# Attention and experts on one core: where q's high parts and the fourth key maximum stand in the order of a block

## The chip, the cores and the metric

The kernel runs on one core of a Trainium2 chip. The metric is the device time of one execution in microseconds (us), taken as the median of several runs. The core has TensorE (PE: matmuls, with its weight loads shown as PEld), VectorE (DVE), ScalarE (ACT), GpSimd (POOL) and SyncE (SP, which issues most DMAs). Each engine works through its own instructions in order, and waits on semaphores for the others.

## What is computed

Two things follow each other, both on x of shape (2, 1024, 256).

```python
# cross attention: 16 heads of 64; queries are the normed x, keys and values the normed context (77) and the normed x
q = lat @ Wq;  k, v = split(concat([x, lat]) @ Wkv)      # per batch: 1024 queries, 1101 keys
attn = softmax(q @ k.T * 64 ** -0.5);  x = x + (attn @ v) @ Wout
# mixture of experts: 32 experts, 4 of them per token through 4 of 8 groups, capacity 320, and one shared expert
x = x + shared(xn) + sum(gate * expert(xn))
```

The change touches only the order of instructions in the attention.

## The kernel before, in words

**Blocks.** The attention is cut into 8 turns T (4 pairs of heads and 2 batches make 16 pairs of heads, two a turn), and each turn into four blocks d = 0 to 3. A block is one pair of heads and 512 queries. I number blocks 4T + d, so 0 to 31. A block walks through two heads (h = 0, 1) and nine key tiles (kt = 0 to 8), which makes 18 slots. In each slot PE makes the scores `st` (a pair of matmuls, lines 939 and 943), ACT takes their exp (L1597, which also frees the PSUM bank for the next scores but one), and POOL adds it to the running sum of the head (`add`, L751).

**Splits.** Projections and scores are made in split float32: a high part and a low part. For q, PE makes the product (`q`, L811, into one of the two banks ps_t), ACT writes four high parts (`hi`, parts 0 to 3, L1574), and then DVE writes two low parts (`lo`, two instructions of L1306), which also frees the bank.

**Maxima.** Softmax needs the row maximum before the exp. For each head and each 128 queries PE multiplies q's high part with all keys (`max`, three matmuls of L916 into the three banks ps_m), and DVE reduces them (L1314) into one column of `neg`. There is only one such set of banks, so each `max` group on PE waits for the reduction of the one before. After four maxima PE turns the columns into a row (`row`, one matmul, L922, into a bank ps_t), and DVE multiplies it in (L1321) where the second score matmul of the head reads it. Right behind the row of head 1 PE makes the sums of the block before (`sum`, L961), whose reciprocal DVE takes (L1325); POOL multiplies it in (`norm`, L756), and PE makes the output (`out`, L974).

**Banks.** The tiles `k`, `q`, `v`, `row`, `sum`, `out` and some routing tiles take the two banks ps_t in turn ("jobs"), and each waits until the job two before it has been read.

**Order.** The order is written out by hand in `turn_slots()`: `after[h, kt]` lists what follows slot (h, kt). `whole_plan()` strings the slots together, and every engine goes through the same plan and picks its own part. Blocks with d odd are *project* blocks: in them the keys, q and values of the next pair of heads are made (`k`, `q`, `v`). Blocks with d even are *light* blocks: only q of the next 512 queries is made. Routing work of the experts is hung on fixed slots of later blocks by `extra_events()`: ("turned", a tile transposed on PE, with its low part on DVE, L1370, in slot (0, 5) of blocks 20 and 24), ("hot_a", a comparison on DVE, L1136, in slot (0, 5) of block 22), ("best_a", a search for the best four, in slot (0, 5) of block 26), and ("scat", an indirect DMA issued by POOL) in slots (0, 2), (0, 7), (1, 2) and (1, 7) of blocks 24 to 31.

**The weights' low part.** In slot (1, 1) of each light block, behind the reciprocal, DVE subtracts the high part of the next Wq and Wk from their raw values (`w`, L1293: both inputs in SBUF, in `arena` and `arena_r`). The next thing that DVE does is the first reduction for the next block.

Of the kernel before, what the change touches and what calls it, by code (L numbers as in the profile page):

```python
# [48 lines left out]
def turn_slots():  # L49


    slots = []
    for d in range(QUADS):
        n, ahead = (d + 1) % QUADS, -int(d == LAST_D)
        prev, behind = (d - 1) % QUADS, int(d == 0)
        pp = n // 2
        project = n % 2 == 0

        def nxt(*ev):
            return ev, ahead  # L60

        def own(*ev):
            return ev, 0

        def old(*ev):
            return ev, behind

        def values(make, block, kts):
            return [make("av", block, kt) for kt in kts]

        def project_q():
            return [nxt("q", pp, n % 2), nxt("hi", "q", pp, n % 2, (0, 1))]

        def project_k(i):
            return [nxt("k", pp, i), nxt("hi", "k", pp, i, (0, 1))]

        q_again, q_low = nxt("hi", "q", pp, n % 2, (2, 3)), nxt("lo", "q", pp, n % 2)
        k_low = [nxt("lo", "k", pp, i) for i in range(3)]
        first_values = values(own, d, (0, 1, 2))
        more_values = values(own, d, (3, 4, 5))  # L80
        last_values = values(old, prev, (6, 7, 8))
        own_max = [own("max", d, 1, i) for i in range(4)]
        next_max = [nxt("max", n, 0, i) for i in range(4)]
        out = [old("out", prev, i) for i in range(2)]
        after = {(0, 8): [own("row", d, 1), old("sum", prev)],
                 (1, 1): [],
                 (1, 2): [old("norm", prev), next_max[0]],
                 (1, 3): first_values + [next_max[1]],
                 (1, 4): [out[0], next_max[2]],
                 (0, 7): last_values[2:]}  # L90
        if project:
            after[0, 0] = [own_max[0]] + project_k(0) + [own_max[1], k_low[0]]
            after[0, 2] = project_k(2) + [own_max[2], k_low[2]]
            after[0, 3] = project_k(1) + [k_low[1]]
            after[0, 5] = project_q() + [q_again] + last_values[:2] + [q_low, own_max[3]]
            after[1, 5] = [nxt("v", pp, 0), next_max[3]]
            after[1, 6] = more_values + [nxt("row", n, 0), out[1]]
            after[1, 7] = [nxt("v", pp, 1)]
            after[1, 8] = [nxt("v", pp, 2)]
        else:  # L100
            after[0, 0] = [own_max[0]] + project_q()
            after[0, 1] = [own_max[1]]
            after[0, 2] = [q_again]
            after[0, 3] = [own_max[2], q_low]
            after[0, 4] = last_values[:2]
            after[0, 5] = [own_max[3]]
            after[1, 6] = [out[1], next_max[3]]
            after[1, 7] = more_values + [nxt("row", n, 0)]
        if d == 0:
            after[1, 1] = [own("w", 1)] + after[1, 1]  # L110
        if d == 2:
            after[1, 1] = [(("w", 0), -1)] + after[1, 1]
        for h in range(2):
            for kt in range(KEY_TILES):
                slots.append([own("st", d, h, kt)] + ([own("add", d, h, kt)] if kt else []) + after.get((h, kt), []))
    return slots
# [98 lines left out]
def whole_plan():  # L215
# [5 lines left out]
              ("max", 0, 0, 1), ("v", 0, 1), ("max", 0, 0, 2), ("v", 0, 2), ("max", 0, 0, 3), ("row", 0, 0)]  # L221
    plan = [(ev, 0) for ev in before]
    slots, extra = turn_slots(), extra_events()
    ahead = [ev for slot in slots for ev, back in slot if back == -1]
    assert set(ahead) <= set(before), set(ahead) - set(before)
# [1476 lines left out]
```

## Time and profile before

| | |
|---|---|
| Time before | 1634.35 us, median of 3 runs (1633.24 to 1637.85) |
| The profiled execution | 1635.06 us, of which 1633.3 us are the span of the records |
| Attention loop | from about 52 us to 1112 us: 32 blocks, a project block about 36.2 us, a light block 28 to 31 us |
| Busy share of the span | PE 93%, weight loads 65%, DVE 64%, POOL 58%, ACT 49% |
| PE clock | granted clock 0.98 of full speed over the span |

The profiled execution is a single one. Busy PE time is made of overlapping matmuls whose ends are modelled, so for PE the distance from start to start says more than the idle times. A start is given in us from the beginning of the span.

### The profile page before, as it was taken

The page shows a single profiled execution, that of the slowest core. Times are in us where ns is not written, and L with a number is a line of the kernel's source. Part 1 is how long each engine was busy: PE and PEld are TensorE (multiplying, and loading weights), DVE is VectorE, ACT ScalarE, POOL GpSimd, SP SyncE. Part 2 cuts the span into 40 slices and gives each one's busy share as a digit, 9 for nine tenths or more (in the row PEclk, how much of TensorE's full clock was granted, in tenths as well). Part 3 has the DMA queues.
Part 4 walks back from the last instruction along what each step waited for, and adds up shares of the span by engine and source line. Part 5 has one row for each costly group of instructions (what it writes and reads, how often), then busy time and mean ns, then how long its engine had stood idle before and what let it go on. Part 6 is the DMA issues. An engine that isn't in the chain of part 4 may idle for free.

```text
span 1633.3 us, 23810 instructions
## 1 busy us (share of the span) xinstructions
PE 1511.4 (93%) x8086; PEld 1060.9 (65%) x8086; DVE 1051.9 (64%) x1574; ACT 798.7 (49%) x1501; POOL 940.4 (58%) x751
## 2 busy tenths in 40 slices
PE   3899999999999999999999999988889999999995
PEld 2565555555655555555555555546779999999995
DVE  6556666576666665767767776556756666666662
ACT  3345444544454445544454444534336666666662
POOL 4457666676566665665668768784433433344333
PEclk8899999999999999999999999999999999999998
DMA  3033440000000000000011000111246666667664
GB/s 95 22 81 72 101 91 11 24 15 10 24 15 10 15 10 24 15 11 15 10 28 32 27 28 27 36 39 59 85 159 175 188 185 169 174 186 188 169 174 89
DMA packets 99282, 117.93 MB, mean 72 GB/s; under 512 B 10595, under 2 KB 78181, under 8 KB 99173
## 3 DMA queue, kind: packets, MB, share of 16 engines
q1 hardware_dynamic: 82149, 96.97, 20.4%
q0 software_dynamic: 17056, 19.97, 6.3%
q8 instruction: 44, 0.72, 0.2%
q14 instruction: 33, 0.27, 0.1%
HBM read 74.93 MB, written 35.06 MB: 67 GB/s over the span
## 4 chain that ended last, share of the span: by engine, by line
PE 66%; DVE 19%; ACT 8%; POOL 3%; issue 3%; DMA 1%; SPq 0%; DVEq 0%; ACTq 0%; POOLq 0%
PE ps_o L954 11%; PE ps_t L811 8%; PE ps_m L811 8%; PE ps_st L811 7%; DVE arena_r L1314 7%; PE ps_m L916 7%; PE ps_st L939 5%; PE ps_st L943 4%; ACT arena_r L1574 3%; PE ps_m L848 3%; PE ps_o L848 3%; DVE arena L1325 2%; PE ps_t L974 2%; PE ps_t L1021 2%; PE ps_t L961 2%
## 5 line engine op out<-in xcount | busy, mean ns | idle before, releaser
L751 POOL TENSOR_TENSOR arena<-arena 128x512 f32<-128x512 f32 (+1 forms) x512 | 660.2, 1291 | 337.7 <-ACT arena L1597 300.2
L1597 ACT ACTIVATE arena<-ps_st 128x512 f32<-128x512 f32 (+1 forms) x576 | 329.9, 596 | 460.8 <-PE ps_st L943 426.4
L1314 DVE TENSOR_REDUCE arena_r<-ps_m 128x1 fp32r<-128x1107 f32 x256 | 334.2, 1306 | 182.8 <-PE ps_m L916 180.7
L786 POOL DMA_INDIRECT acc_rows<-arena,ids x96 | 150.8, 1571 | 268.1 <-ACT arena L1660 240.4
L954 PE MATMUL ps_o<-arena 128*64 128x512 f32 (+1 forms) x1152 | 276.5, 606 | 0.0
L939 PE MATMUL ps_st<-arena_r 128*128 128x512 f32 (+1 forms) x576 | 247.2, 429 | 13.9 <-ACT arena L1597 13.9
L943 PE MATMUL ps_st<-arena_r 68*128 68x512 f32 (+2 forms) x576 | 231.1, 401 | 2.5 <-DVE arena_r L1321 1.4
L916 PE MATMUL ps_m<-arena_r 128*128 128x370 f32 x768 | 192.6, 359 | 34.6 <-DVE arena_r L1314 27.1
L916 PEld LDWEIGHTS ps_m<-arena_r 128*128 128x128 f32 x768 | 130.9, 192 | 109.5 <-DVE arena_r L1314 68.5
L939 PEld LDWEIGHTS ps_st<-arena_r 128*128 128x128 f32 (+1 forms) x576 | 106.8, 185 | 108.1 <-ACT arena L1597 83.5
L811 PE MATMUL ps_m<-arena_r 128*128 128x320 f32 (+1 forms) x864 | 164.7, 326 | 2.1 <-DVE arena_r L1404 1.2
L954 PEld LDWEIGHTS ps_o<-arena 128*64 128x64 f32 (+1 forms) x1152 | 71.6, 136 | 139.3 <-issue 131.6
L811 PE MATMUL ps_st<-arena_r 128*128 128x320 f32 (+1 forms) x864 | 159.6, 320 | 0.0
L811 PEld LDWEIGHTS ps_m<-arena_r 128*128 128x128 f32 x864 | 136.1, 190 | 13.5 <-issue 9.8
L1448 DVE TENSOR_TENSOR arena<-arena,ps_st 128x320 f32<-128x320 f32 x128 | 62.1, 485 | 125.1 <-ACT arena L1635 125.1
L811 PEld LDWEIGHTS ps_st<-arena_r 128*128 128x128 f32 x864 | 137.3, 189 | 4.2
L1434 DVE TENSOR_TENSOR arena_r<-arena,arena_r 128x1024 fp32r<-128x1024 f32 x93 | 113.7, 1222 | 15.7 <-ACT arena_r L1622 12.5
L943 PEld LDWEIGHTS ps_st<-arena_r 68*128 68x128 f32 (+2 forms) x576 | 107.0, 186 | 18.1 <-DVE arena_r L1321 10.4
L1325 DVE RECIPROCAL arena<-ps_t 128x512 f32<-128x512 f32 x32 | 107.4, 3357 | 11.7 <-PE ps_t L961 11.7
L811 PE MATMUL ps_t<-arena_r 128*128 128x512 f32 x384 | 105.0, 411 | 4.5 <-DVE arena_r L1303 2.6
L1635 ACT ACTIVATE arena<-ps_m 128x320 f32<-128x320 f32 x128 | 56.3, 440 | 102.7 <-PE ps_st L811 100.4
L1321 DVE TENSOR_TENSOR arena_r<-ps_t,mask 4x512 fp32r<-4x512 f32 x64 | 43.8, 684 | 86.3 <-PE ps_t L922 86.2
(211 smaller groups left out, 1922.7 us busy)
## 6 DMA issues: line engine op xcount, KB each, us to landing
arena<-in_L_ffn_wg_dram SPq DMA_DIRECT2D x32, 512.0 KB, 4.6
arena<-in_L_ffn_wu_dram SPq DMA_DIRECT2D x32, 512.0 KB, 6.3
arena<-in_L_ffn_wd_dram SPq DMA_DIRECT2D x32, 512.0 KB, 3.8
x_slots<-route SPq DMA_DIRECT2D x5, 2176.0 KB, 12.9
arena<-x_slots SPq DMA_DIRECT2D x32, 272.0 KB, 2.7
arena_r<-arena_r SPq DMA_DIRECT2D x30, 275.2 KB, 3.8
arena<-in_L_xattn_Wkv_dram SPq DMA_DIRECT2D x32, 128.0 KB, 2.4
arena<-x_slots SPq DMA_DIRECT2D x32, 68.0 KB, 2.4
```

The source lines that it names most:

```text
L751: pool.tensor_tensor(total, probsT[0:rows, h, 0, :] if kt == 1 else total, probsT[0:rows, h, kt, :], ALU.add).then_inc(added, 1)
L786: pool.indirect_dma_start(out=dst[:, :], in_=y_sb[par][:, c, 0:w], in_offset=None, compute_op=ALU.add, out_offset=bass.IndirectOffsetOnAxi ...
L811: mm = pe.matmul(ps, a, m, start=(n == 0), stop=(n == len(pairs) - 1))
L848: mm = pe.matmul(banks[c], a, m, start=(k == 0 and n == 0), stop=(k == HT - 1 and n == 2))
L916: mm = pe.matmul(ps_m[:, piece, 0:PIECE_W + 1], q1[h][:, c:c + P], k1[pp][h][:, lo:lo + PIECE_W + 1], start=True, stop=True)
L939: pe.matmul(ps_st[0:rows, n % 2, :], k1[pp][h][:, r], q1[h][:, c:c + 512], start=True, stop=False)
L943: pe.matmul(ps_st[0:rows, n % 2, :], k2[pp][h][kr, r], q2[h][kr, c:c + 512], start=False, stop=True).then_inc(st_ready, 1)
L954: mm = pe.matmul(ps_o[ROWK[h], :], vals[0:rows, d // 2, kt, ROWK[h]], probsT[0:rows, h, kt, :], start=(kt == 0), stop=(kt == KT_N - 1), sk ...
L1314: dve.tensor_reduce(neg[h][:, c:c + 1], ps_m[:, :, 0:PIECE_W], AX.XY, ALU.max, negate=True)\
L1325: dve.reciprocal(rinv[:, :], bank[:, :]).then_inc(free, 1)
L1434: dve.tensor_tensor(ws_lo[slot][piece], w_raw[slot][:, piece * W:(piece + 1) * W], ws_hi[slot][piece].bitcast(F32), ALU.subtract).then_inc ...
L1597: act.activation(probsT[0:rows, h, kt, :], ps_st[0:rows, n % 2, :], ACT.Exp).then_inc(exp_done, 1)
```

## The change

The change rewrites two parts of the table `after`, and defines `q_high`, a list of the four high parts of q as four events of one instruction each (before there were two events with two instructions each).

```diff
+        q_high = [nxt("hi", "q", pp, n % 2, (part,)) for part in range(4)]
...
             after[0, 3] = project_k(1) + [k_low[1]]
-            after[0, 5] = project_q() + [q_again] + last_values[:2] + [q_low, own_max[3]]
+            after[0, 4] = [own_max[3]]
+            after[0, 5] = project_q() + [q_again] + last_values[:2] + [q_low]
...
         else:
-            after[0, 0] = [own_max[0]] + project_q()
-            after[0, 1] = [own_max[1]]
-            after[0, 2] = [q_again]
-            after[0, 3] = [own_max[2], q_low]
-            after[0, 4] = last_values[:2]
-            after[0, 5] = [own_max[3]]
+            after[0, 0] = [own_max[0], nxt("q", pp, n % 2)]
+            after[0, 1] = [own_max[1], q_high[0]]
+            after[0, 2] = [q_high[1]]
+            after[0, 3] = [own_max[2]]
+            after[0, 4] = last_values[:2] + q_high[2:]
+            after[0, 5] = [own_max[3], q_low]
```

No instruction is added or removed. Because of two new lines above them, everything stands two lines lower in the changed kernel (L1314 becomes L1316, and so on).

**Project blocks, DVE.** From the third maximum of head 1 to the reciprocal, in block 5. L1303 are low parts of k, L1314 the reductions, L1306 the low parts of q, L1321 the row's multiply. Before:

```order
L1314 TENSOR_REDUCE arena_r<-ps_m 128x1
L1303 TENSOR_TENSOR arena_r<-ps_t,arena_r 64x77 x2
L1303 TENSOR_TENSOR arena_r<-ps_t,arena_r 64x512 x2
L1306 SCALAR_TENSOR_TENSOR arena_r<-ps_t,arena_r 64x512 x2
L1314 TENSOR_REDUCE arena_r<-ps_m 128x1
L1321 TENSOR_TENSOR arena_r<-ps_t,mask 4x512
L1325 RECIPROCAL arena<-ps_t 128x512
```

And in the changed kernel:

```order
L1305 TENSOR_TENSOR arena_r<-ps_t,arena_r 64x512 x2
L1316 TENSOR_REDUCE arena_r<-ps_m 128x1
L1308 SCALAR_TENSOR_TENSOR arena_r<-ps_t,arena_r 64x512 x2
L1323 TENSOR_TENSOR arena_r<-ps_t,mask 4x512
L1327 RECIPROCAL arena<-ps_t 128x512
```

The fourth reduction now stands ahead of q's low parts. On PE its three matmuls stand between the scores (0, 4) and (0, 5); before, they stood behind q and the values (0, 6) and (0, 7).

**Light blocks, ACT.** The exps (L1597) and q's high parts (L1574) from the last exp of the block before, in one light block. Before:

```order
L1597 ACTIVATE arena<-ps_st 128x512
L1574 ACTIVATE arena_r<-ps_t 64x512 x2
L1597 ACTIVATE arena<-ps_st 128x512 x2
L1574 ACTIVATE arena_r<-ps_t 64x512 x2
L1597 ACTIVATE arena<-ps_st 128x512 x5
```

And in the changed kernel:

```order
L1599 ACTIVATE arena<-ps_st 128x512 x2
L1576 ACTIVATE arena_r<-ps_t 64x512
L1599 ACTIVATE arena<-ps_st 128x512
L1576 ACTIVATE arena_r<-ps_t 64x512
L1599 ACTIVATE arena<-ps_st 128x512 x2
L1576 ACTIVATE arena_r<-ps_t 64x512 x2
L1599 ACTIVATE arena<-ps_st 128x512 x3
```

The second exp of the block now stands ahead of all high parts, the third behind one, and the fourth behind two. PE's order in light blocks is the same as before.

**Light blocks, DVE.** The reductions, q's low parts and the row's multiply of one light block. Before:

```order
L1314 TENSOR_REDUCE arena_r<-ps_m 128x1 x3
L1306 SCALAR_TENSOR_TENSOR arena_r<-ps_t,arena_r 64x512 x2
L1314 TENSOR_REDUCE arena_r<-ps_m 128x1
L1321 TENSOR_TENSOR arena_r<-ps_t,mask 4x512
L1325 RECIPROCAL arena<-ps_t 128x512
```

And in the changed kernel:

```order
L1316 TENSOR_REDUCE arena_r<-ps_m 128x1 x4
L1308 SCALAR_TENSOR_TENSOR arena_r<-ps_t,arena_r 64x512 x2
L1323 TENSOR_TENSOR arena_r<-ps_t,mask 4x512
L1327 RECIPROCAL arena<-ps_t 128x512
```

Here q's low parts moved the other way: behind the fourth reduction, right ahead of the row's multiply.

## Rows read from the trace of the kernel before

**Rows 1.** The page, part 1: busy us, share of the span, instructions
```profile
PE 1511.4 (93%) x8086; PEld 1060.9 (65%) x8086; DVE 1051.9 (64%) x1574; ACT 798.7 (49%) x1501; POOL 940.4 (58%) x751
```
**Rows 2.** The waits, attention loop: total us, times, longest us
```profile
PE ps_m L916 <- DVE arena_r L1314: 26.1, 28, 1.9
PE ps_st L939 <- ACT arena L1597: 13.9, 38, 1.3
```
**Rows 3.** The timeline, PE, project block 9: start, us, what, [idle before]
```profile
358.29 0.45 PE L939 MATMUL ps_st<-arena_r 128*77 128x512 f32 x1
...
359.19 0.47 PE L922 MATMUL ps_t<-ident,arena_r 128*128 128x512 f32 x1 [0.21 <-DVE arena_r L1314]
359.59 1.08 PE L961 MATMUL ps_t<-arena,ones 128*64 128x512 f32 x4
```
**Rows 4.** The timeline, DVE, same block
```profile
356.31 1.39 DVE L1306 SCALAR_TENSOR_TENSOR arena_r<-ps_t,arena_r 64x512 fp32r<-64x512 f32 x2 [2.12 <-ACT arena_r L1574]
357.73 1.31 DVE L1314 TENSOR_REDUCE arena_r<-ps_m 128x1 fp32r<-128x1107 f32 x1
```
**Rows 5.** The timeline, PE, light block 10, same place
```profile
391.65 0.45 PE L939 MATMUL ps_st<-arena_r 128*77 128x512 f32 x1
...
392.50 1.08 PE L961 MATMUL ps_t<-arena,ones 128*64 128x512 f32 x4
```
**Rows 6.** Line 1306: what DVE waited for ahead of it, us, times
```profile
  ACT arena_r L1574: 32.2, 15
```
**Rows 7.** The timeline, PE, light block 2, maxima two and three
```profile
120.83 0.40 PE L943 MATMUL ps_st<-arena_r 68*128 68x512 f32 x1
...
122.65 0.50 PE L939 MATMUL ps_st<-arena_r 128*128 128x512 f32 x1 [0.46 <-ACT arena L1597]
...
123.22 0.69 PE L916 MATMUL ps_m<-arena_r 128*128 128x370 f32 x3
```
**Rows 8.** The timeline, DVE and ACT, same stretch
```profile
121.77 1.31 DVE L1314 TENSOR_REDUCE arena_r<-ps_m 128x1 fp32r<-128x1107 f32 x1 [1.05 <-PE ps_m L916]
...
122.00 1.09 ACT L1597 ACTIVATE arena<-ps_st 128x512 f32<-128x512 f32 x2
```
**Rows 9.** The timeline, light block 2, fourth maximum and the sums
```profile
127.46 1.31 DVE L1314 TENSOR_REDUCE arena_r<-ps_m 128x1 fp32r<-128x1107 f32 x1 [0.91 <-PE ps_m L916]
...
130.19 1.08 PE L961 MATMUL ps_t<-arena,ones 128*64 128x512 f32 x4
```
**Rows 10.** The timeline, blocks 20 (two rows) and 22
```profile
721.90 0.69 DVE L1370 TENSOR_TENSOR arena_r<-ps_t,arena_r 128x512 fp32r<-128x512 f32 x1
...
723.29 1.08 PE L961 MATMUL ps_t<-arena,ones 128*64 128x512 f32 x4
...
789.76 1.38 DVE L1136 TENSOR_TENSOR spare<-topf,iota_e 128x512 f32<-128x512 f32 x1
```
**Rows 11.** The timeline, POOL, light block 2, its first adds
```profile
122.68 6.95 POOL L751 TENSOR_TENSOR arena<-arena 128x512 f32<-128x512 f32 x5 [2.66 <-ACT arena L1597]
```
**Rows 12.** The timeline, the weights' low part, blocks 2 and 10
```profile
134.59 1.10 DVE L1293 TENSOR_TENSOR arena_r<-arena,arena_r 128x512 fp32r<-128x512 f32 x1
...
396.90 0.63 DVE L1293 TENSOR_TENSOR arena_r<-arena,arena_r 128x512 fp32r<-128x512 f32 x1
396.93 1.72 POOL L751 TENSOR_TENSOR arena<-arena 128x512 f32<-128x512 f32 x1
```
**Rows 13.** The timeline, blocks 28 (two rows) and 30
```profile
998.16 3.19 DVE L1293 TENSOR_TENSOR arena_r<-arena,arena_r 128x512 fp32r<-128x512 f32 x1
...
1002.63 0.61 PE L916 MATMUL ps_m<-arena_r 128*128 128x370 f32 x2 [1.94 <-DVE arena_r L1314]
...
1069.93 1.10 PE L974 MATMUL ps_t<-wout_sb,arena 128*128 128x256 f32 x4 [1.71 <-POOL arena L756]
```
**Rows 14.** The timeline, PE, third maximum ahead, blocks 6 and 10
```profile
269.87 0.79 PE L916 MATMUL ps_m<-arena_r 128*128 128x370 f32 x3 [1.70 <-DVE arena_r L1314]
...
402.84 0.44 PE L916 MATMUL ps_m<-arena_r 128*128 128x370 f32 x1 [1.38 <-DVE arena_r L1314]
```

## The prediction

> **What bounds the kernel now.** I read the page first: PE is busy 93% of the span, no other engine over 64% [rows 1]. So only PE's own idle time can be won, and an edit that moves no PE work can help only where PE waits. Then the view of waits over the attention loop: PE waits 26.1 us for the reductions of maxima and 13.9 us for exps [rows 2]. Small sums, but the waits are regular, so I went through the timeline of one block of each kind, and looked for the same waits in the others. The reader is to see three chains beside PE: ACT's exps, DVE's reductions, and POOL's adds.
>
> **Project blocks: the fourth maximum.** In block 9 the ninth score pair of head 0 starts at 358.29 and the sums at 359.59: 1.30 us [rows 3]. In light block 10 the same stretch takes 392.50 - 391.65 = 0.85 us [rows 5]. The 0.45 us between them is the row's wait: q's low parts hold DVE from 356.31 for 1.39 us, and only then comes the fourth reduction, 357.73 to 359.04 [rows 4]; the row's matmul starts at 359.19. After the change the reduction stands ahead of q's low parts and ends over 3 us before the row needs it. DVE waits 15 times for q's high parts, 32.2 us together [rows 6]: these are the 15 blocks with d odd that make a next q (block 31 makes none). 15 x 0.45 = **6.7 us less**. Lower bound: the printed idle time, 0.21 x 15 = 3.2 us.
> What is late next? PE's product for q starts one max group later (about 0.6 us), so q's low parts start near 357.0 and end near 358.4. The row's multiply can start near 359.2. The cover is 0.8 us, and it would have to be gone before this costs anything.
>
> **Light blocks, the direct part.** In block 2 PE waits 0.46 us for an exp [rows 7], because two exps stand behind two high parts on ACT and start only at 122.00 [rows 8]. The change removes this wait in 11 blocks (the light ones but 0, 8, 10, 12, 14, where DVE is late instead). But the score pair is followed by the third max group, and that needs the second reduction, which ends at 121.77 + 1.31 = 123.08 [rows 8]. It starts at 123.22 today [rows 7]. So at most 0.14 us can come back, and a max group that had to wait lasts 0.79 [rows 14] where this one lasts 0.69 [rows 7]. Between 0 and 0.14 x 11 = 1.5 us I take **0**.
>
> **Light blocks, q's low parts.** They move behind the fourth reduction. In block 2 this ends at 127.46 + 1.31 = 128.77; 1.39 us more [rows 4], with the usual small overlap, gives about 130.1. The sums use the bank that they free, and start at 130.19 [rows 9]. So they fit by less than 0.1 us: 0 in the plain blocks, and the first thing to check. It doesn't fit where more stands there:
> - Block 20: a turned tile stands between, so the row takes q's bank and the sums the tile's. The tile's low part starts at 721.90 and lasts 0.69; behind q's low parts it ends at 721.90 + 1.38 + 0.69 = 723.97, plus 0.07 until PE sees it, against sums at 723.29 [rows 10]. **0.75 us more.**
> - Block 22: the comparison at 789.76, 1.38 long [rows 10], moves back too. It has two inputs in SBUF and has to get past POOL's adds (below). Between 0.2 and 3.5 us; I take **1.5 us more**.
> - Block 0 is irregular (PE starts cold): between a gain of 0.2 and a loss of 2; **0.7 us more**.
>
> **POOL and the weights' low part.** This part isn't in the diff. The first add of block 2 starts at 122.68, as soon as its second exp is done, and then adds follow each other for 6.95 us [rows 11]: 1.28 each and 0.14 apart. The second exp's scores end at 120.83 + 0.40 [rows 7]; it can start near 121.3 and not at 122.00. So POOL's chain of adds starts 0.7 us earlier. Who waits for it? L1293 has both inputs in SBUF, as the adds have, and the rows show that one waits for the other: 0.63 us in block 10, where it starts 0.03 us before an add, which then takes 1.72 for 1.28; 1.10 in block 2, where it comes into a running add [rows 12]; 3.19 in block 28, where the indirect DMAs have put POOL behind and two adds follow each other without a gap [rows 13]. So DVE gets in only between adds that have a gap between them.
> - Blocks 24, 26, 28: POOL is behind from the first add on, so 0.7 us earlier there is 0.7 us earlier here. PE waits 1.94 for it in block 28 [rows 13], so it is passed on. Block 24 has the turned tile of block 20 and block 26 a search in the same slot, so their reciprocals come 0.75 and up to 1.4 later; but there L1293 waits for the adds until later than that anyway (3.1 us in block 26), so POOL sets the time. Block 30: PE's output waits 1.71 for POOL's multiply [rows 13]; the same 0.7. Together 0.5 + 3 x 0.7 = **2.6 us less**.
> - Blocks 4, 6, 16, 18: in them the adds catch up with the sixth exp, whose time isn't moved, as in block 10. I expect the 0.63 of block 10 and not 1.10. Block 6 against 10 shows the worth: 1.70 - 1.38 = 0.32 [rows 14]. For the four, by what else waits there, 0.2 + 0.3 + 0.4 + 0.6 = **1.5 us less**. In block 2 PE has 0.1 us of slack there: 0. Blocks 8 to 14 already have it.
>
> **Sum.** Against the profiled execution's own 1635.06: -6.7 + 0 + 0.75 + 1.5 + 0.7 - 2.6 - 1.5 = -7.9, so 1627.2. The median of the runs is 0.7 lower than this execution; I say **1627 us**.
>
> **Rivals.**
> - *Nearly nothing moves.* The project term is at its lower bound (3.2), the adds bring nothing, and blocks 0, 20 and 22 cost more than I took (3.0): 1635.06 - 0.2, about 1634. For it: the three costs are in places where I had to bound. Against: the 0.45 repeats itself in all 15 blocks.
> - *Only the printed idle time comes back.* PE's idle time ahead of the row is printed as 0.21, half of what the starts show [rows 3]. If a wait costs no more than this, because the row's weights are loaded while PE waits, the project term is 3.2 and the time 1635.06 - 7.9 + 3.5 = 1631. Against it: 0.45 is the same work from start to start, with and without the wait. The Trainium skill, page "TensorE: Matmul & The Clock Gate", section "Architectural detail: the array is 16× 32×32, not 1× 128×128", says that PE's queue can pull weight loads ahead of running matmuls, which speaks for this case.
> - *The light part pays in full.* If the third max group were not held by the reduction, 11 x 0.46 = 5.1 us more would go: 1622. Against it stands 123.08 against 123.22.
> - *Slower: DVE misses the gap.* In block 10 the weights' low part starts 0.03 us ahead of an add [rows 12]. After the change I expect this state in nine blocks. If q's low parts push the sums back by more than that, the reciprocal and L1293 come just after the add has started; and behind it stand POOL's multiply and another add without a gap, so that DVE waits some 3 x 1.28 = 3.8 us and not 0. In block 28 such a wait reached PE nearly in full. At 3 us in eight blocks: 1627 + 24 = 1651. It decides at a push of 0.03 us; my slack for the sums is under 0.1. Slower than before from three such blocks on. The Trainium skill, page "SBUF — State Buffer", section "SBUF: two separate sides", states for such pairs that whoever starts first gets the port for its whole instruction and the other fully blocks; the trace agrees as far as the add of 1.72 us goes, which lost 0.44 to an instruction of 0.63.
>
> **How the numbers follow.** Forecast (5 to 12 us less): 0.55. Only the printed idle time: 0.08. Nearly nothing: 0.15. Light part in full: 0.07. Missed gaps: 0.15. What a measurement of this kernel can tell from no change is about 0.3%, 4.9 us. Faster by more: 0.55 + 0.07 = 0.62; the same: 0.08 + 0.15 = 0.23; slower: 0.15. Range: from the light part in full (1622) over the forecast to four missed gaps on top of it (1627 + 12 = 1639). This leaves out the worse half of the missed gaps and less than 0.05 below. The forecast's own range is 1623 to 1630.
>
> **What would show it.** Right: in project blocks 0.85 us from the last score pair to the sums. In light blocks the exp's wait is gone and the third max group starts when it does now, waiting for DVE. The sums of plain light blocks follow their row by 0.33 as now. In block 20 they start 0.75 later. L1295 (now L1293) has a median near 0.63 and a maximum near 2.5, no longer 3.2. Wrong: L1295 with times of 3 to 4 us in blocks that had 0.6 or 1.1 (missed gaps), a new wait of the sums or of the second score matmul behind q's low parts, or a wait of q's product's readers that delays the row in project blocks.

## The result, and the profile after

The changed kernel takes 1622.6 us (median of 4 runs, 1621.29 to 1625.27) against 1634.8 for the kernel before: a ratio of 0.9923, 95% interval 0.991 to 0.9936. That is 12.2 us less; 1627 had been forecast, and 5 to 12 us less as the forecast's own range, which the measured time leaves by 0.2 us. The profiled execution took 1625.27 us, its span is 1623.5 us. In the tables below a block's length is the time from PE's first score matmul of the block to that of the next; block 31 ends with the first matmul of the experts' shared part. "The loop" is the sum over the 32 blocks: 1059.77 us before and 1052.37 in this execution.

The page of the kernel after, part 1, in the columns of [rows 1]:

```profile
PE 1509.4 (93%) x8086; PEld 1061.8 (65%) x8086; DVE 1044.7 (64%) x1574; ACT 799.2 (49%) x1501; POOL 940.2 (58%) x751
```

PE's busy time fell by 2.0 us and the span by 9.8, so most of what went is idle time. The view of PE's waits over the loop of the kernel after (total us, times, longest us) says which:

```profile
PE ps_m L918 <- DVE arena_r L1316: 26.5, 36, 1.6
PE ps_st L941 <- ACT arena L1599: 8.3, 26, 1.3
```

The wait for exps fell from 13.9 us to 8.3 [rows 2]. The wait for reductions didn't fall, 26.1 to 26.5, but it occurs 36 times and not 28: in the light blocks the one turned into the other.

**Project block 9.** The timeline of the kernel after, PE, from the last score pair (its first matmul) to the sums:

```profile
359.01 0.46 PE L941 MATMUL ps_st<-arena_r 128*77 128x512 f32 x1
...
359.55 0.40 PE L924 MATMUL ps_t<-ident,arena_r 128*128 128x512 f32 x1
359.88 1.08 PE L963 MATMUL ps_t<-arena,ones 128*64 128x512 f32 x4
```

From pair to sums 0.87 us, where it was 1.30 [rows 3] and 0.85 had been forecast. The row has no wait. DVE's timeline of the same stretch shows why, and that q's low parts, one max group later, have room:

```profile
354.94 1.31 DVE L1316 TENSOR_REDUCE arena_r<-ps_m 128x1 fp32r<-128x1107 f32 x1
357.55 1.39 DVE L1308 SCALAR_TENSOR_TENSOR arena_r<-ps_t,arena_r 64x512 fp32r<-64x512 f32 x2 [1.29 <-ACT arena_r L1576]
359.99 0.68 DVE L1323 TENSOR_TENSOR arena_r<-ps_t,mask 4x512 fp32r<-4x512 f32 x1 [1.05 <-PE ps_t L924]
```

The fourth reduction ends at 356.25, 3.3 us ahead of the row. The low parts end at 358.94, and DVE is idle for 1.05 us before the row's multiply. In all 15 odd blocks from 1 to 29 the distance from pair to sums went from 1.29 to 1.31 us to 0.85 to 0.87.

The weights of the row's matmul are the columns `neg`, which the reductions write, so the wait holds the weight load too. The load of the row in block 9, first before, then after:

```profile
359.16 0.19 PEld L922 LDWEIGHTS ps_t<-ident,arena_r 128*128 128x128 f32 x1 [0.65 <-issue]
```

```profile
359.31 0.19 PEld L924 LDWEIGHTS ps_t<-ident,arena_r 128*128 128x128 f32 x1
```

Before, it starts 0.03 us ahead of the row's matmul. After, it starts 0.24 us ahead of it, while the score matmul in front still runs. These 0.21 us are most of the difference between the printed idle time (0.21) and the 0.43 to 0.45 us that the wait cost from start to start.

**Light block 2.** PE's timeline after, in order the second group of maxima, the score pair behind which the exp's wait of 0.46 us stood [rows 7], and the third group:

```profile
123.78 0.67 PE L918 MATMUL ps_m<-arena_r 128*128 128x370 f32 x3
124.29 0.39 PE L941 MATMUL ps_st<-arena_r 128*128 128x512 f32 x1
...
124.75 0.44 PE L941 MATMUL ps_st<-arena_r 128*128 128x512 f32 x1
...
125.86 0.78 PE L918 MATMUL ps_m<-arena_r 128*128 128x370 f32 x3 [0.42 <-DVE arena_r L1316]
```

The exp's wait is gone, and the third group waits for DVE instead. The block took 28.09 us before and takes 28.08.

**The weights' low part.** It is L1295 now. DVE and POOL of the kernel after in block 2, then in block 28:

```profile
137.31 0.63 DVE L1295 TENSOR_TENSOR arena_r<-arena,arena_r 128x512 fp32r<-128x512 f32 x1
...
137.35 1.71 POOL L753 TENSOR_TENSOR arena<-arena 128x512 f32<-128x512 f32 x1
...
992.80 2.52 DVE L1295 TENSOR_TENSOR arena_r<-arena,arena_r 128x512 fp32r<-128x512 f32 x1
```

In block 2 it took 1.10 before [rows 12] and now meets the gap ahead of an add, as it did in block 10; in block 28 it waits 0.67 us less than in [rows 13].

**Block 0** is what went otherwise. It was 30.00 us long and is 33.42 in this execution. DVE, POOL (a row that holds two adds) and then PE of the kernel after:

```profile
68.54 1.82 DVE L1295 TENSOR_TENSOR arena_r<-arena,arena_r 128x512 fp32r<-128x512 f32 x1 [2.23 <-ACT arena_r L1565]
...
73.34 1.12 DVE L1269 TENSOR_SCALAR spare<-spare,cstat 40x256 f32<-40x256 f32 x1
...
68.47 3.03 POOL L753 TENSOR_TENSOR arena<-arena 77x512 f32<-77x512 f32 x2
...
74.67 0.22 PE L968 MATMUL ps_t<-ident,spare 40*128 40x40 f32 x1 [1.51 <-DVEq L1271]
75.98 1.29 PE L918 MATMUL ps_m<-arena_r 128*128 128x370 f32 x3 [1.09 <-DVE arena_r L1316]
77.07 0.63 PE L941 MATMUL ps_st<-arena_r 128*128 128x512 f32 x1
```

L1295 lasts 1.82 us here (0.80 before). PE waits twice for over 1 us, where before it waited 0.32 and 1.09, and behind the second wait a score matmul takes 0.63 us and not 0.40. L1269 isn't what is new: it took 1.15 us before. The windows of the two kernels over this place, first of before, then of after (from:to, length, PE, PEld, DVE, ACT, POOL busy, **granted clock**, DMA share, GB/s):

```profile
68.00:76.00 8.00, 6.58 (x30) 3.62 (x30) 6.16 (x10) 2.44 (x5) 7.43 (x6) 1.00 0.00 1
76.00:84.00 8.00, 7.62 (x34) 4.00 (x33) 3.82 (x5) 2.87 (x5) 5.25 (x5) 1.00 0.00 0
```

```profile
68.00:76.00 8.00, 5.40 (x26) 2.52 (x24) 7.16 (x9) 2.19 (x4) 7.15 (x6) 0.94 0.00 1
76.00:84.00 8.00, 8.00 (x25) 4.53 (x25) 2.85 (x4) 1.79 (x3) 3.82 (x3) 0.63 0.00 0
```

The clock falls from the full 2.4 GHz to half of it during the second wait (1.00 between 74 and 75 us, 0.55 between 75 and 76, with PE busy for 0.02 us of it), and stays there for most of the second window, a mean of 0.63.

### The profile page after: what moved, and what is told of

Its sections match the earlier page's. It is cut to its first block, busy times and chain, and to the rows that moved or that the text cites. A ratio compares the mean times of both kernels' runs of the same rounds, so it can differ in the third digit from the quotient of the medians.

```text
span 1623.5 us, 23810 instructions
## 1 busy us (share of the span) xinstructions
PE 1509.4 (93%) x8086; PEld 1061.8 (65%) x8086; DVE 1044.7 (64%) x1574; ACT 799.2 (49%) x1501; POOL 940.2 (58%) x751
## 4 chain that ended last, share of the span: by engine, by line
PE 75%; DVE 17%; ACT 4%; POOL 2%; issue 2%; DMA 1%; DVEq 0%; SPq 0%; ACTq 0%; POOLq 0%
PE ps_o L956 14%; PE ps_t L813 9%; PE ps_m L918 8%; PE ps_m L813 8%; PE ps_st L813 7%; DVE arena_r L1316 7%; PE ps_st L941 6%; PE ps_st L945 5%; PE ps_m L850 3%; PE ps_o L850 3%; PE ps_t L976 2%; PE ps_t L1023 2%; PE ps_t L963 2%; DVE arena_r L1305 1%; DVE arena L1327 1%
## 5 line engine op out<-in xcount | busy, mean ns | idle before, releaser
L1316 DVE TENSOR_REDUCE arena_r<-ps_m 128x1 fp32r<-128x1107 f32 x256 | 334.1, 1305 | 201.2 <-PE ps_m L918 199.2
L1624 ACT ACTIVATE arena_r<-arena 128x1024 fp32r<-128x1024 f32 x93 | 98.3, 1057 | 1.4 <-DMA arena<-in_L_ffn_wu_dram 1.4
```

What stands on the lines that cost most here:

```text
L1316: dve.tensor_reduce(neg[h][:, c:c + 1], ps_m[:, :, 0:PIECE_W], AX.XY, ALU.max, negate=True)\
L1624: act.activation(ws_hi[slot][piece], w_raw[slot][:, piece * W:(piece + 1) * W], ACT.Copy)\
```

## The experiments

Each kernel was timed beside the kernel before on one chip. Runs of before alone lie between 1630.3 and 1638.2 us, with a granted clock of 0.987 in the shortest and 0.979 in the longest, so a median of few runs says less than a block's length: outside blocks 0 and 31 that repeats within a few hundredths of a us, as long as the clock is at 1.00 in it. This table, worked out from the starts of PE's matmuls (sums over many blocks are good to 0.04), gives for one execution of each kernel what the blocks gained or lost against before, in us. "Odd" are the 15 project blocks 1 to 29, "plain" is 2, 8, 10, 12, 14.

| kernel | block 0 | odd | plain | 4, 6, 16, 18 | 20 | 22 | 24 to 30 | 31 | loop |
|---|---|---|---|---|---|---|---|---|---|
| changed | +3.42 | -6.62 | -0.16 | -1.72 | +0.68 | +0.05 | -2.60 | -0.45 | -7.40 |
| after_again | -0.33 | -6.65 | -0.09 | -1.76 | +0.65 | +0.04 | -2.57 | -1.30 | -12.01 |
| p_only | -0.08 | -6.70 | -0.02 | +0.01 | 0.00 | +0.01 | +1.78 | -0.39 | -5.39 |
| l_only | +2.14 | +0.09 | -0.13 | -1.71 | +0.67 | +0.01 | -2.62 | +1.01 | -0.54 |
| block0_old | +0.10 | -6.74 | -0.14 | -1.78 | +0.66 | +0.01 | -2.55 | +0.12 | -10.32 |
| qlow_first | +1.79 | -6.62 | -0.14 | -1.75 | +0.09 | -0.24 | -2.76 | -1.36 | -10.99 |
| low_late | -0.05 | -6.45 | -0.05 | -0.02 | +0.62 | +0.68 | +0.04 | +0.96 | -4.27 |
| w_late | -0.73 | -4.21 | -3.12 | -3.52 | -0.23 | -0.01 | -4.01 | +1.02 | -14.81 |
| value_first | +3.52 | -6.63 | -1.12 | -2.46 | +0.30 | +0.03 | -2.73 | +0.87 | -8.22 |
| pad2 | +2.12 | -6.72 | +1.01 | -0.88 | +0.95 | +0.19 | -1.37 | +0.35 | -4.35 |
| w_qlow | +1.37 | -4.04 | -3.94 | -3.44 | -0.81 | -0.22 | -4.72 | +2.50 | -13.30 |
| all_three | +1.60 | -4.97 | -2.73 | -3.65 | -0.29 | +0.03 | -3.96 | -0.32 | -14.29 |

Some entries are the clock's. In these 13 traces it is below 1.00 in block 0 of each, in block 31 of all but after_again and qlow_first (the two whose block 31 is 1.3 us shorter), and elsewhere only in blocks 26 and 28 of p_only, 27 of w_late and w_qlow, and 26 of pad2. In all other blocks it is 1.00.

**1. The project blocks' edit alone** (p_only). Against the kernel before:

```diff
-            after[0, 5] = project_q() + [q_again] + last_values[:2] + [q_low, own_max[3]]
+            after[0, 4] = [own_max[3]]
+            after[0, 5] = project_q() + [q_again] + last_values[:2] + [q_low]
```

> The kernel before with the project blocks' edit alone (the fourth maximum two slots up; light blocks as before). Theory: this edit gives nearly all of the gain, about 0.45 us in each of the 16 project blocks, so the attention loop ends 6.7 to 7.2 us earlier and the kernel takes about 1627.5 us; the light blocks keep their lengths within 0.05 us. Rival, that the light blocks' edit carries the gain beside it and the two only work together: under 3 us here, 1631 or more.

Measured: 1630.86 us, ratio 0.9981 (0.9968 to 0.9995). Each odd block is 0.43 to 0.47 us shorter, as in the changed kernel, so the term stands. The loop is only 5.4 us shorter since blocks 26 and 28 came out 0.51 and 1.27 longer, though nothing in them was edited. That is the clock and no interaction of the edits. The windows in p_only, and those of the same places before:

```profile
929.00:932.00 3.00, 2.92 (x7) 2.02 (x8) 2.56 (x3) 0.66 (x2) 2.83 (x3) 0.50 0.12 46
997.00:1000.00 3.00, 3.00 (x10) 2.43 (x9) 1.31 (x1) 0.60 (x1) 2.82 (x3) 0.50 0.14 46
```

```profile
935.00:938.00 3.00, 1.97 (x9) 1.47 (x10) 2.69 (x4) 0.70 (x2) 2.83 (x3) 1.00 0.12 46
1003.00:1006.00 3.00, 3.00 (x15) 2.22 (x14) 2.32 (x3) 0.60 (x1) 2.81 (x3) 1.00 0.14 46
```

Up to these places the two blocks keep step with those of before, with the same waits, and in one execution the clock falls while in the other it stays. Without these 1.8 us the loop would be 7.2 us shorter. The profiled execution is the shortest of its ten. By the median the rival would have held (1631 or more); the blocks decide for the theory.

**2. The light blocks' edit alone** (l_only). Against the changed kernel it is the diff of experiment 1 read backwards.

> The changed kernel with the project blocks' order as before, so the light blocks' edit alone. Theory: its gains and losses nearly cancel: block 0 +3.4 us, block 20 +0.7, blocks 4, 6, 16, 18 and 24 to 30 together -4.3, the plain ones 0; the attention loop stays within 1 us of before and the kernel at about 1634. Rival, that the part of the measured gain that my sum did not have comes from the light blocks: 1630 or less. What neither part explains (some 2 us behind the attention loop) would then show in both kernels or in neither.

Measured: 1633.06 us, ratio 0.9987 (0.9972 to 1.0002), which is no difference clear of noise; loop -0.54. Outside blocks 0 and 31 the theory holds block by block: the light blocks are those of the changed kernel, the odd ones those of before. Over blocks 1 to 30 the two edits add up: -3.7 us here and -6.7 in p_only without the clock's 1.8 us make -10.4, and the changed kernel has -10.4 in both of its executions.

**3. Block 0 in its old order** (block0_old). The slots of the first turn get, in block 0 alone,

```diff
+                after[0, 0] = [own_max[0], nxt("q", pp, n % 2)] + q_high[:2]
+                after[0, 1] = [own_max[1]]
+                after[0, 2] = q_high[2:]
+                after[0, 3] = [own_max[2], q_low]
+                after[0, 4] = last_values[:2]
+                after[0, 5] = [own_max[3]]
```

> The changed kernel, but block 0 keeps its order of before (q's low part in one step behind the maxima). Theory: in block 0 the low part comes up while GpSimd's two adds stand back to back, DVE misses the gap, and TensorE then loses 2.2 us waiting and 1.2 us in a stretch at the lower clock; so block 0 returns from 33.4 to 30.0 us and the kernel gains 3.4 us, to about 1619. Rival, that block 0's extra is the new order as such (exps waiting in any order) or the start-up of the stage, whichever way it is ordered: under 1 us gained.

Measured: 1626.1 us, ratio 0.995 (0.9932 to 0.9967). Block 0 is back at 30.10 us, and L1295's counterpart lasts 0.89 us in it. The time of the whole, forecast at 1619, didn't fall below the changed kernel's; the next experiment says why.

**4. The changed kernel once more** (after_again), without an edit.

> The changed kernel once more, beside the others of this group on one chip. Theory, that the attention loop's 7.4 us and a stretch behind it that differs from execution to execution make the time: the loop's length comes out at 1052.4 us again, within 0.3, while the ratio to before lies nearer 0.995 than 0.992. Rival, that the change does something behind the loop as well: the stretch from the loop's end to the last matmul stays at 502.4 us, 2.2 shorter than before, and the ratio stays at 0.992.

Measured: 1624.31 us, ratio 0.9933 (0.991 to 0.9956). The forecast of the loop was wrong: it is 1047.75 us and not 1052.4. All blocks but two repeat; block 0 is 29.67 us long in this execution and was 33.42 in the other, and block 31 differs by 0.85, with the clock at 1.00 in it here and at 0.62 between 1076 and 1084 us there. DVE and POOL of this execution in block 0 (the POOL rows are two adds):

```profile
67.34 0.69 DVE L1295 TENSOR_TENSOR arena_r<-arena,arena_r 128x512 fp32r<-128x512 f32 x1 [2.23 <-ACT arena_r L1565]
...
66.00 1.28 POOL L753 TENSOR_TENSOR arena<-arena 128x512 f32<-128x512 f32 x1
...
67.43 1.73 POOL L753 TENSOR_TENSOR arena<-arena 77x512 f32<-77x512 f32 x1
```

Here L1295 starts 0.06 us behind the end of an add and 0.09 ahead of the next, and takes 0.69 us; in the other execution it started 0.07 us behind the start of an add and took 1.82. It waits for ACT (the 2.23 us in brackets). That ACT's time hangs on when the clock rises is my reading and isn't tested: the granted clock between 52 and 60 us is 0.72 here and was 0.62 there. In this execution the clock stays at 1.00 behind 68 us:

```profile
68.00:76.00 8.00, 6.41 (x29) 3.37 (x29) 6.67 (x11) 2.28 (x4) 6.79 (x6) 1.00 0.00 1
76.00:84.00 8.00, 7.92 (x35) 4.32 (x34) 3.31 (x3) 2.46 (x5) 4.57 (x4) 1.00 0.00 1
```

PE's waits in the same place are

```profile
72.18 0.22 PE L968 MATMUL ps_t<-ident,spare 40*128 40x40 f32 x1 [0.21 <-DVEq L1271]
73.49 0.78 PE L918 MATMUL ps_m<-arena_r 128*128 128x370 f32 x3 [1.09 <-DVE arena_r L1316]
```

0.21 and 1.09 us, where they were 1.51 and 1.09 in the other execution. So the 3.75 us between the two are 0.2 us before 68.6, 1.3 us of the first wait, and 2.2 us of the stretch at the lower clock, between 76 and 84.3 us.

So the +3.4 us of block 0 don't come in every execution of this order, but the order bears on them. Ten traces keep L1295 where it was. In the four with block 0 in its old order (before, p_only, block0_old, low_late) L1295 takes 0.69 to 0.89 us and block 0 is 29.9 to 30.1 us long, though their granted clock between 52 and 60 us is only 0.57 to 0.62. Of the six with the high parts in their new places one is like them (after_again, the one with the highest clock there, 0.72); in the changed kernel, l_only, value_first, pad2 and qlow_first L1295 takes 1.43 to 2.04 us and block 0 is 31.8 to 33.5 us long, at 0.59 to 0.68. Six traces can't say how often the new order goes well. The rival here, that the stretch behind the loop stays at 502.4 us, fell too: from the loop's end to the last matmul it is 505.0 us, against 504.6 before. Over all traces it lies between 501.1 and 505.1, whatever the kernel.

**5. q's low part ahead of the fourth maximum** (qlow_first), light blocks:

```diff
-            after[0, 5] = [own_max[3], q_low]
+            after[0, 5] = [q_low, own_max[3]]
```

> The changed kernel, but in the light blocks q's low part stands ahead of the fourth maximum instead of behind it. Theory A, that the fourth maximum's place decides in plain light blocks: the last exps wait 0.6 us more in each of 9 blocks, +5 us in all, while blocks 20 and 24, where q's turned tile waits for the low part, give 0.4 to 0.7 us each back. Theory B, that only the end of the low part matters: -1.5 us and nothing lost in the plain blocks.

Measured: one run, 1624.39 us. Theory B: nothing lost in the plain blocks, 0.59 us back in block 20, 0.29 in 22, 0.15 in 24. In block 0 the row then waits 1.03 us, and the clock's mean between 68 and 76 us is 0.79; the two kernels of 9 and 10 that share this order show the same (1.04 and 0.79).

**6. q's high parts as before, the low part late** (low_late). Against the changed kernel, light blocks:

```diff
-            after[0, 0] = [own_max[0], nxt("q", pp, n % 2)]
-            after[0, 1] = [own_max[1], q_high[0]]
-            after[0, 2] = [q_high[1]]
+            after[0, 0] = [own_max[0], nxt("q", pp, n % 2)] + q_high[:2]
+            after[0, 1] = [own_max[1]]
+            after[0, 2] = q_high[2:]
             after[0, 3] = [own_max[2]]
-            after[0, 4] = last_values[:2] + q_high[2:]
+            after[0, 4] = last_values[:2]
```

> The changed kernel, but in the light blocks q's high parts come as before, two steps behind the first group of maxima and two behind the third tile; only the low part stays behind the fourth maximum. Theory: the 4.3 us that blocks 4, 6, 16, 18 and 24 to 30 lose come from the low part's new place alone, which moves VectorE's work against GpSimd's adds; the split high parts only turn the exp's wait of 0.62 us into a wait of 0.59 us of the third maximum. So block lengths stay within 0.1 us of the changed kernel's (block 0 apart, which comes out at 29.7 or at 32 to 33.5 by chance), with the exp's wait back in each light block. Rival, that the split high parts carry the gain: blocks 4, 6, 16, 18, 24 to 30 return to their lengths of before, loop +4 us.

Measured: one run, 1631.12 us, loop -4.27. My theory of this run fell, and its rival holds: blocks 4, 6, 16, 18 and 24 to 30 are back at their lengths of before, within 0.04 us each. Their gain of 4.3 us comes from the high parts, which no longer hold ACT ahead of the exps, and not from the low part's place; qlow_first, with the low part ahead of the fourth maximum, keeps it (-1.75 and -2.76). That is what the prediction had said, and what I had turned round when I wrote this expectation. PE's and DVE's timelines of this kernel in block 2 show both halves: the exp's wait is back, and L1295 comes into a running add (133.12 to 134.39 in the trace) and lasts 1.09 us, as it did before.

```profile
121.90 0.50 PE L941 MATMUL ps_st<-arena_r 128*128 128x512 f32 x1 [0.46 <-ACT arena L1599]
...
133.84 1.09 DVE L1295 TENSOR_TENSOR arena_r<-arena,arena_r 128x512 fp32r<-128x512 f32 x1
```

Block 22 is 0.68 longer in this kernel and 0.05 in the changed one: there the late low part alone does cost (the comparison takes 1.48 us), and with the earlier adds it takes 0.84 and the cost is gone.

**7. Two small instructions ahead of q's low part** (pad2), light blocks:

```diff
                     dve.wait_ge(pair_hi, HI_N[ev[1:], T])
+                    for _ in range(2 if which == "q" and i == 1 else 0):
+                        seq.done(dve.memset(pad[:, :], 0.0))
+                        seq.wait()
```

> The changed kernel with two empty waits and memsets of one element each on VectorE ahead of q's low part in the light blocks, some 0.2 us together, which push what stands behind. Theory, the missed gap: VectorE's subtraction for the weights' low part starts 0.2 us later, misses the 0.14 us between GpSimd's two adds in blocks where it now meets it, and lasts 1.5 to 4 us instead of 0.63 to 0.75; PE then waits for the maxima and the loop gets 3 us longer or more. Rival, that it isn't the gap that the first 0.6 us hit: durations stay at 0.63 to 0.75 and the loop changes by less than 1 us.

Measured: one run, 1631.37 us. The plain blocks are 0.2 us longer each, all of the delay that I had put in, and in them L1295 takes 0.63 us still. In block 2 it starts at 136.26, 0.04 us ahead of an add, as in the changed kernel: the add has moved by the same 0.2 us. What I had taken for the point where the missed gap decides, a push of 0.03 us, is refuted for the plain blocks: what delays the sums delays PE, PE's scores delay the exps, and the exps delay POOL. It also shows that the low part had no slack ahead of the sums, since all of the 0.2 us came out. Of the theory the mechanism fell and the size came true, the rival the other way round: over blocks 1 to 30 the kernel is 3.5 us longer than the changed one. Block 26 alone is 0.9 of this, with the clock at 0.51 between 926 and 929 us.

**8. The weights' low part late** (w_late). Against the changed kernel:

```diff
-            after[1, 1] = [own("w", 1)] + after[1, 1]
+            after[1, 6] = [own("w", 1)] + after[1, 6]
         if d == 2:
-            after[1, 1] = [(("w", 0), -1)] + after[1, 1]
+            after[1, 6] = [(("w", 0), -1)] + after[1, 6]
```

> The changed kernel with the subtraction that makes the weights' low part moved from the second half's second tile to its seventh in the light blocks, behind the next block's first maxima on VectorE instead of ahead of them. Theory: where it missed GpSimd's gap, in blocks 0, 20, 24, 26, 28 (1.4 to 2.5 us), and where the third maximum of the next block waits 1.7 us (blocks 6, 8, 10, 12), it held the reductions; moved, these blocks lose 0.5 to 1.2 us each, block 0 2 to 3 us: the loop is 6 to 9 us shorter than the changed kernel's. Rival, that the wait sits in the reductions' own chain and the subtraction only fills it: under 1.5 us.

Measured: 1619.89 us, ratio 0.9909 (0.9887 to 0.9931); after_again, in the same group, has 1624.31. Blocks 6, 8 and 12 are 1.3 us shorter than the changed kernel's, 26 is 1.1 and 20 is 0.9 shorter: there the subtraction did hold the reductions, and PE's wait for them falls from 26.5 us to

```profile
PE ps_m L918 <- DVE arena_r L1316: 18.4, 31, 2.0
```

The light blocks 2 to 30 are 7.1 us shorter together. Against these stand 2.4 us in blocks 19, 21, 23 and 27, so that without blocks 0 and 31 the loop is 4.7 us shorter than the changed kernel's. That is less than I had expected, for a reason that DVE's and POOL's rows in block 27 of this kernel show:

```profile
928.95 2.44 DVE L1174 TENSOR_TENSOR route<-route 128x32 f32<-128x32 f32 x3
...
929.03 0.99 POOL L775 DMA_INDIRECT x_slots<-kvT,slot  x1
930.04 1.29 POOL L753 TENSOR_TENSOR arena<-arena 77x512 f32<-77x512 f32 x1
```

Three routing instructions of some 0.2 us each take 2.44 us together: the third starts at 929.41 and ends at 931.40, behind an indirect DMA and an add of POOL. PE then waits 1.97 us for the second reduction of that block, where it waited 1.26: the same wait, on another DVE instruction. It accounts for 0.7 of the 1.5 us of block 27; the other 0.8 are the clock, at 0.53 between 934 and 937 us. In all_three, with the same wait and the clock at 1.00, the block loses 0.7.

**9 and 10. The moves put together.** w_qlow is experiment 8 with experiment 5; all_three adds value_first (11) to them.

> The changed kernel with two of the moves tried: the weights' low part at the second half's seventh tile, q's low part ahead of the fourth maximum. Theory, that the gains add: 6.2 us in blocks 6 to 30 and about 3 in block 0 from the first, 1.0 in blocks 20, 22 and 24 from the second; loop 1044 us against 1052.4 or 1047.8 of the changed kernel, time 1618. Rival, that the second only moved VectorE against GpSimd and falls away with the first: loop 1045, as the first alone.

> The two moves of the kernel beside this one, and the value matmuls around the third maximum as well. Theory: the latter gave 0.2 us in 12 light blocks and 0.35 in block 20, and adds to the others: loop 1041.5 us, time 1615.5 to 1616. Rival, that with the weights' low part late, VectorE takes up what TensorE wins: loop 1044, no faster than the kernel beside it.

Measured: w_qlow 1620.61 us, ratio 0.9908 (0.9892 to 0.9924); all_three 1619.18 us, ratio 0.9892 (0.9876 to 0.9909). In w_qlow the gains add in blocks 10, 20, 22 and 24 (2.3 us over w_late together), but block 0 loses 2.1 us by the row's wait and the lower clock behind it, block 31 came out 1.5 us longer with a clock of 0.86, and nothing is left. By the times neither rival can be excluded, since the intervals overlap. The blocks say more. Over blocks 1 to 30 w_late is at -15.1 us, w_qlow at -17.2 and all_three at -15.6, the first two with 0.8 us of the clock's in block 27. So the second move does add to the first. The third takes back more than it gives: beside w_qlow, blocks 8, 12 and 24 lose 0.6 to 0.7 us each. all_three has the lowest median of the study, 3 to 5 us below the changed kernel's (1622.6 and 1624.3), but it can't be told from w_late and w_qlow.

**11. Value matmuls around the third maximum** (value_first). Against the changed kernel, light blocks:

```diff
-            after[0, 3] = [own_max[2]]
-            after[0, 4] = last_values[:2] + q_high[2:]
+            after[0, 3] = last_values[:1] + [own_max[2]]
+            after[0, 4] = last_values[1:2] + q_high[2:]
```

> The changed kernel with one group of the previous block's value matmuls put ahead of the third maximum and one behind it in the light blocks. Theory: the third maximum's group waits 0.59 us in every light block because the reduction of the group before it holds the bank, and no work stands between; a group of value matmuls fills it: 0.4 to 0.6 us less in each of 14 light blocks, loop 6 to 8 us shorter. Rival, that the exps bound the half block and the wait only moves behind: the exps then wait the same 0.6 us later on and the loop changes by less than 1 us.

Measured: 1623.7 us, ratio 0.9923 (0.9899 to 0.9948). PE's timeline of this kernel, block 2: value matmuls stand ahead of the third group, and no idle time is printed for it.

```profile
124.38 1.08 PE L956 MATMUL ps_o<-arena 128*64 128x512 f32 x4
125.39 0.78 PE L918 MATMUL ps_m<-arena_r 128*128 128x370 f32 x3
```

But the block is 0.2 us shorter and not 0.4 to 0.6. Of the third maximum's wait the larger part turns up again later in the block. Neither theory holds as I wrote it: over blocks 1 to 30 the kernel is 2.3 us shorter than the changed one. In the time of the whole this doesn't show (1623.7 beside after_again's 1624.31).

## Why the prediction was right, and where it wasn't

The direction, the mechanism and most sizes held; the time is 4.4 us below the forecast, at the range's lower end. By the time alone the rival "the light part pays in full" (1622) would be nearer than the forecast; it is the blocks that refute it. Term by term, with the two executions of the changed kernel:

- **Project blocks, -6.7.** Measured -6.62 and -6.65, and -6.70 with this edit alone. The rival of the printed idle time is refuted: PE's idle time ahead of the row is printed as 0.21 [rows 3] and 0.44 us came back per block. Its condition, that the row's weights are loaded while PE waits, doesn't hold: the load starts only 0.03 us ahead of the matmul, since its weights are what the reduction writes. That PE's queue can pull weight loads ahead of running matmuls, as the Trainium skill states ("TensorE: Matmul & The Clock Gate", section "Architectural detail: the array is 16× 32×32, not 1× 128×128"), therefore speaks for nothing here; the trace agrees with it only where the weights are ready, as after the change, where the load starts 0.24 us ahead. Block 31 was rightly left out: its distance from pair to sums is 0.86 us before and after.
- **Light blocks, direct, 0.** -0.16 and -0.09 in the plain ones. The exp's wait turned into one of the third maximum, as worked out, so "the light part pays in full" fell. Experiment 11 puts a price on it: with work put into the wait, 0.2 us a block.
- **q's low parts, 0 in plain blocks.** Right, and with no slack at all (experiment 7).
- **Block 20, +0.75.** +0.68 and +0.65.
- **Block 22, +1.5: mis-sized.** +0.05 and +0.04. The comparison took 1.38 us [rows 10] because it came into an add; behind the low parts it takes 0.84, and that this is owed to the earlier adds low_late shows (1.48 us, block +0.68).
- **Block 0, +0.7: mis-sized, in a way that one number can't mend.** It is +3.42 or -0.33. I had bounded the loss at 2 and had counted neither a missed gap there nor the clock, which falls in the waits behind it and makes up 2.2 of the 3.75 us.
- **POOL's adds, -2.6 and -1.5.** -2.60 and -2.57 in blocks 24 to 30; -1.72 and -1.76 in 4, 6, 16, 18. L1295 takes 0.63 us in 6, 16 and 18 and 0.75 in block 4. This was the part furthest from the diff, and low_late and qlow_first confirm its cause.
- **Missed gaps, the slower rival.** In the plain light blocks it didn't happen, since POOL's adds move with the sums. In block 0 it did, by another trigger than the one that I had named, and never at the 3.8 us of the working: L1295 took 1.82 us there. Its premise, that DVE gets in only between adds with a gap, fell too: in block 0 it got in between two adds without one.

The sum for the loop was -7.9; it measured -7.40 and -12.01. The difference between the two is block 0 (3.75 us) and block 31 (0.85). That the first comes so near is luck: block 0 was 2.7 us worse than its term, and block 22, block 31 and the smaller terms made up for it. The median is 12.2 us below before, the second profiled execution's span 12.6 (1633.3 to 1620.7), the first one's 9.8. In the second execution the loop is 4.2 us below the sum: block 22 (1.5), block 31 (1.3), block 0 where it goes well (1.0), and 0.4 us of small terms. The median's 4.4 us fit this, but which way block 0 went in the runs without a trace isn't known.

The two parts alone give -3.5 and -1.3 us in the medians, less than half of what they give together. In blocks 1 to 30 they add up to within 0.1 us, so this isn't the order; the times of p_only's ten runs go with the granted clock, from 1626.6 us at 0.983 to 1633.9 at 0.977. An estimate from straight lines through time and clock of the runs of that group, read at 0.982, gives -6.0 and -3.4 us. What stays open: why the clock falls in the same wait in one execution and not in another, and how often block 0 goes either way.

## What to carry to other kernels

Measure a regular wait from start to start against a like block that doesn't have it; the printed idle time gave half of what came back, because the weights of the matmul behind the wait were late as well. An edit that takes work from in front of a chain's first link (here the exps) is worth more in the blocks where the chain's last link (here POOL) is late than where the wait is printed. Where two engines exclude each other, a shift that moves both did no harm here; the danger is where their triggers differ, as in block 0, where one waits for ACT. Look there first, and look at more than one execution. Before a block that nobody edited is called an interaction, read the granted clock in it.

## What the runs showed of the hardware

A DVE subtraction with both inputs in SBUF (L1295) and POOL's adds exclude each other, and when depends on hundredths of a us. Started 0.04 us ahead of an add it takes 0.63 us, and the add 1.71 for 1.28: the add loses 0.43 and not the subtraction's whole 0.63. Started 0.07 us behind an add's start it takes 1.82 us, which is the add's remaining 1.21 (68.54 to 69.75, the add's end worked out from its start and duration) and its own 0.61. For such pairs the Trainium skill, page "SBUF — State Buffer", section "SBUF: two separate sides", says that who comes first has the port for the whole instruction. The second case agrees. In the first the add was held for 0.43 us, though 0.59 of the subtraction's 0.63 us were left when it started, so the measured hold is shorter than the whole instruction. Whether DVE gets in between two adds that follow without a gap isn't settled by these runs: in block 0 of the changed kernel it did (1.82 us, and the second add was lengthened), in block 28 it waited through such a pair (2.52 us).

PE's granted clock fell in a wait: in block 0 of the changed kernel, behind a wait of 1.51 us and during one of 1.09. Its mean between 76 and 84 us is 0.63, and a score matmul took 0.63 us for 0.40, with nothing to wait for. In the other execution, where the first wait is 0.21 us and the second 1.09 as well, the clock stays at 1.00. Of block 0's 3.75 us between the two executions 2.2 are this, and not the wait that set it off. The same waits don't always bring it about: in blocks 26 and 28 of p_only the clock fell to 0.50, and in the same places before it stayed at 1.00.
